# An attention and mixture-of-experts layer: rotation moved behind the q and k projections, and small uses moved to other slots

## The chip, the cores and the metric

The kernel runs on one core of one Trainium2 chip. The metric is the device time of one execution in microseconds. Three executions of the kernel before took 602.74, 608.37 and 611.11 us; their median is 608.37 us.

## The reference, cut to what matters

The input x has 8 batches of 512 tokens of width 128. One layer is differential attention with rotary positions, a residual sum and layer norm, then a top-1 mixture of 8 experts, a residual sum and layer norm.

```python
q = apply_rope((x @ Wq).reshape(B, T, 32, 4), cos, sin)      # x1*c + x2*s, -x1*s + x2*c
k = apply_rope((x @ Wk).reshape(B, T, 16, 4), cos, sin)      # halves of a head: d = 0,1 and 2,3
v = (x @ Wv).reshape(B, T, 8, 2, 4)
attn = softmax(q1 k1 / 2, causal) v - lambda_full * softmax(q2 k2 / 2, causal) v
attn = attn / rms(attn) * rms_w * (1 - LAMBDA_INIT)
x = layernorm(x + attn @ Wo)
max_prob, expert = top1(softmax(x @ router_w + router_b))
x = layernorm(x + max_prob * silu(x @ w1a[expert]) * (x @ w1g[expert]) @ w2[expert])
```

## The kernel before, in words

**Phases.** The attention part is a pipeline of `PHASES` = 34 phases. A phase g handles one group of head pairs, and four groups (`SUPER` = 4) make a batch, so phases come in fours: g%4 = 0, 1, 2, 3. A phase has nine slots t, each with two steps u. In each step TensorE writes one bank of scores in natural order for group g (`nat_mask`, `nat_part`, L681 and L699), whose row maxima VectorE takes (`row_max`, L1431), and one bank of transposed scores for group g-2 (`st_mask`, `st_part`, L718), which ScalarE turns into exponentials (`exp`, L980). In most slots the products with v follow (`pv`, L766). There are three banks for natural scores (`nat_b`), four for transposed ones (`st_b`) and one for the products with v (`pv_b`).

**Small uses.** At the end of a slot TensorE does what `uses(g, t)` lists, before that slot's `pv`. `PAIR_USES` come in every phase: `turn_max` in slot 2 (turns the row maxima, L803) and `turn_ot` in slot 4 (L809). `BATCH_USES` prepare the next batch b: q in two halves of 256 tokens ("q" in slot 6 and "q2" in slot 8 of phase 4b-4), k in two halves ("k" in slot 2 and "k2" in slot 6 of phase 4b-3), and v in slot 2 of phase 4b-2. `CHAIN` places the steps after the attention of a batch (output projection `wo`, `turn_x1`, `router`, `rank`, and GpSimd's `norm` and `sort`) as (phases after 4b, slot), and `JOBS` VectorE's small steps as (phases after 4b, step u, count).

**Rotation before.** GpSimd multiplies the transposed input `xt_s` by four rows of cosines and sines (`turn`, L1144, four products into `xr` in slots 0 to 3 of phase 4b-4). A half of q is then eight products on TensorE (`project`, L777 and L783): four column groups of 32, each the sum of a product with `wq_s[:, 2a]` and one with the weights of exchanged columns. ScalarE copies each half to `rot` (L1023). GpSimd splits `rot` into three bf16 parts (`split`, L1157 to L1163, slots 0 to 3: q in phase 4b-3, k in phase 4b-2). The SP queue writes the parts to `qk_parts` in DRAM (`write_part`, L533, six transfers per tensor) and reads them back as operands for each group (`operands`, `load_rows`, L548). It also sends the turned maxima out and in (`max_out` L568, `max_in` L575), all in one order per phase. The first batch is projected before the phases begin.

**Warm products.** In phases 0 and 1, and twice in phase 2, `warm_slot` adds products with no use of their own (L854, 512 columns) at the end of a slot: two per slot, none where a half of q or k stands.

**After phase 33** come the experts: 23 slots of rows with 256 x 128 products in f32 (`hidden` L909, `down` L924).

## Time and profile before

| | us |
|---|---|
| median of 3 executions (lowest, highest) | 608.37 (602.74, 611.11) |
| the profiled execution, its own time | 604.31 |
| its span, first to last instruction | 602.5 |
| TensorE busy | 573.8 (95%) |
| VectorE busy | 502.4 (83%) |
| ScalarE busy | 428.8 (71%) |
| GpSimd busy | 334.5 (56%) |
| mean granted clock of TensorE | 0.977 |

The busy time of TensorE contains the time in which a matmul passes through the array, so back-to-back products count as fully busy. Times of instructions are from the span's start. A phase is bounded here by the end of VectorE's last reduction of the phase (L1441); phase 0 begins at about 23.8 us and phase 31 ends at 455.7 us. The granted clock has two levels, 1.00 (2.4 GHz) and 0.50 (1.2 GHz).

### The profile page before, as it was taken

The numbers are of one execution on the slowest core, as the hardware profiler recorded it, in microseconds if no ns is written. First come the engines' busy times: TensorE is split into PE (matmuls) and PEld (weight loads), VectorE is DVE, ScalarE is ACT, GpSimd is POOL, SyncE is SP. The second block draws the span as 40 slices with busy tenths as digits, with TensorE's granted clock in tenths as the row PEclk, the third lists the DMA queues.
The fourth block names the chain that finished last, engine by engine and source line by source line (L and its number), as shares of the span: only waits on it lengthen the run. The fifth ranks groups of instructions, "written<-read, shape, count | busy, mean of one in ns | idle before, by whom it ended". The sixth has DMA issues, their size and how long they took to land.

```text
span 602.5 us, 30974 instructions
## 1 busy us (share of the span) xinstructions
PE 573.8 (95%) x12993; PEld 340.9 (57%) x13001; DVE 502.4 (83%) x1250; ACT 428.8 (71%) x903; POOL 334.5 (56%) x569
## 2 busy tenths in 40 slices
PE   7989999999999999999999999999999999999995
PEld 2434454555554555455445545555555588899995
DVE  4487898998999899899989998999996678866665
ACT  4115788998887888889888878889888845344443
POOL 5322033773577386739755773863265404866576
PEclk9977899999999999999999999999999999999998
DMA  3703312421341333234113412422110884698710
GB/s 107 188 10 111 101 36 77 119 54 35 92 113 41 88 94 90 57 85 116 41 50 91 117 43 76 107 68 57 35 26 24 277 262 153 208 316 260 256 56 35
DMA packets 44083, 62.85 MB, mean 104 GB/s; under 512 B 13436, under 2 KB 35196, under 8 KB 43800
## 3 DMA queue, kind: packets, MB, share of 16 engines
q1 hardware_dynamic: 38888, 54.31, 31.0%
q0 software_dynamic: 2416, 5.08, 2.4%
q8 instruction: 102, 1.67, 1.2%
q10 hardware_dynamic: 2640, 1.48, 1.0%
q14 instruction: 37, 0.30, 0.2%
HBM read 42.79 MB, written 21.65 MB: 107 GB/s over the span
## 4 chain that ended last, share of the span: by engine, by line
PE 56%; DVE 20%; POOL 15%; issue 6%; ACT 2%; DMA 1%; POOLq 0%; DVEq 0%; ACTq 0%
DVE mr L1431 14%; PE bank L766 13%; PE bank L909 9%; PE bank L681 7%; PE bank L699 7%; PE bank L924 4%; PE bank L777 3%; POOL x_all L1264 3%; PE bank L854 3%; PE bank L783 3%; PE bank L718 2%; PE bank L809 2%; PE bank L819 1%; PE bank L828 1%; POOL out_dram L1323 1%
## 5 line engine op out<-in xcount | busy, mean ns | idle before, releaser
L1431 DVE TENSOR_REDUCE mr<-bank 128x8 f32<-128x512 f32 x576 | 363.6, 681 | 43.5 <-PE bank L699 40.9
L980 ACT ACTIVATE work<-bank 128x512 f32<-128x512 f32 x576 | 313.1, 599 | 55.7 <-PE bank L718 49.4
L766 PE MATMUL bank<-work,v_aug 128*32 128x256 f32 (+6 forms) x2560 | 172.8, 370 | 0.0
L699 PE MATMUL bank<-kd,qd 24*64 24x192 bf16 (+7 forms) x2048 | 163.4, 289 | 0.0
L718 PE MATMUL bank<-qd,kd 27*64 27x320 bf16 (+7 forms) x2048 | 160.1, 286 | 0.0
L681 PEld LDWEIGHTS bank<-bits 32*64 32x64 bf16 x4608 | 76.7, 104 | 130.6 <-DVE mr L1431 63.5
L681 PE MATMUL bank<-bits 32*64 32x64 bf16 (+2 forms) x4608 | 131.4, 211 | 10.4 <-DVE mr L1431 7.0
L766 PEld LDWEIGHTS bank<-work,v_aug 128*32 128x32 f32 x2560 | 62.4, 110 | 58.3 <-issue 23.2
L1174 POOL CAST msplit<-mt 128x32 bf16<-128x32 f32 x32 | 6.8, 213 | 118.0 <-DVE mt L1441 118.0
L699 PEld LDWEIGHTS bank<-kd,qd 24*64 24x64 bf16 x2048 | 66.6, 109 | 0.1
L718 PEld LDWEIGHTS bank<-qd,kd 27*64 27x64 bf16 x2048 | 65.3, 108 | 0.0
L1100 ACT ACTIVATE sa<-bank 128x256 f32<-128x256 f32 (+1 forms) x92 | 30.9, 349 | 37.7 <-PE bank L909 29.6
L1276 POOL DMA_INDIRECT x_sorted<-x_all,pos_u x32 | 32.1, 1003 | 32.6 <-DVE pos_u L1521 25.1
L1323 POOL DMA_INDIRECT out_dram<-ynorm,row_u x39 | 39.4, 1009 | 11.9 <-issue 8.9
L1144 POOL TENSOR_TENSOR xr<-xt_s,rope 128x512 f32<-128x512 f32 x28 | 34.7, 1273 | 8.6 <-DMA xt_s<-in_xT 8.6
L1764 DVE TENSOR_TENSOR u_s<-sa,bank 128x256 f32<-128x256 f32 (+1 forms) x92 | 31.9, 375 | 7.4 <-ACT sa L1100 7.0
L909 PE MATMUL bank<-xr,wbuf 128*128 128x256 f32 (+1 forms) x176 | 35.5, 353 | 1.8 <-DVE xr L1720 0.7
L909 PE MATMUL bank<-xr,work 128*128 128x256 f32 (+1 forms) x192 | 37.1, 346 | 0.1
L909 PEld LDWEIGHTS bank<-xr,work 128*128 128x128 f32 x192 | 31.2, 191 | 3.4 <-DVE xr L1720 0.4
L909 PEld LDWEIGHTS bank<-xr,wbuf 128*128 128x128 f32 x176 | 29.1, 191 | 5.4 <-DVE xr L1720 1.1
L1082 ACT ACTIVATE ynorm<-ymix,shift,rstd 128x128 f32<-128x128 f32 x37 | 16.4, 486 | 19.8 <-DMA out_dram<-ynorm,row_u 15.7
L1333 POOL TENSOR_TENSOR rstd<-var,half 128x2 f32<-128x2 f32 (+1 forms) x23 | 15.5, 674 | 16.3 <-DVE var L1746 15.8
(206 smaller groups left out, 734.7 us busy)
## 6 DMA issues: line engine op xcount, KB each, us to landing
qk_parts<-parts SPq DMA_DIRECT2D x91, 128.0 KB, 2.4
work<-in_w SPq DMA_DIRECT2D x12, 768.0 KB, 6.1
wbuf<-in_w SPq DMA_DIRECT2D x11, 768.0 KB, 6.7
kd<-qk_parts SPq DMA_DIRECT2D x64, 96.0 KB
qd<-qk_parts SPq DMA_DIRECT2D x62, 96.0 KB
x_sorted<-in_c_pad SPq DMA_DIRECT2D x9, 390.0 KB, 4.6
xr<-x_sorted SPq DMA_DIRECT2D x16, 130.0 KB, 2.8
xt_s<-in_xT SPq DMA_DIRECT2D x8, 256.0 KB, 3.9
```

The lines of the kernel that those rows point to most:

```text
L681: pe.matmul(bk[L * c:L * c + L, :].rearrange("p (n t) -> p n t", t=L)[:, first:first + step * (wide - 1) + 1:step, cols], unit_h[lo:lo + L ...
L699: m = pe.matmul(bk[L * c:L * c + L, cols], qd[lo:lo + KROWS, s % 2, second, c, L * n:L * n + L], kd[lo:lo + KROWS, s % 2, second, c, 0:key ...
L718: m = pe.matmul(bk[L * c:L * c + L, cols], kd[lo:lo + KROWS + MAXROWS, s % 2, second, c, L * n:L * n + L], qd[lo:lo + KROWS + MAXROWS, s % ...
L766: m = pe.matmul(pv_b[32 * t:32 * t + 32, lo:hi], v_aug[:, vb, kv + v, kb, :], prob[:, pos, r, lo - back:hi - back], start=piece == 0, stop ...
L909: m = pe.matmul(banks[f][:, h * SLOT:h * SLOT + P * WIDE[j]], w_slots[j % WRING][:, h * FFN + f * P:h * FFN + (f + 1) * P], xst[:, n % 2, ...
L980: nc.scalar.activation(prob[:, pos, r, :], st_b[no % ST_RING][:, :], ACT.Exp, scale=HD ** -0.5).then_inc(s_sfree, 1)
L1100: nc.scalar.activation(sa[:, f, 0:P * WIDE[j]], banks[f][:, 0:P * WIDE[j]], ACT.Silu).then_inc(s_silu, 1)
L1144: nc.gpsimd.tensor_tensor(xr[:, i, :], xt_s[:, :], rope[:, i, :], ALU.mult).then_inc(s_xr, 1)
L1276: nc.gpsimd.indirect_dma_start(out=x_sorted, out_offset=bass.IndirectOffsetOnAxis(pos_u[:, n:n + 1], 0), in_=x1_all[:, n, :], in_offset=None)\
L1323: nc.gpsimd.indirect_dma_start(out=out, out_offset=bass.IndirectOffsetOnAxis(row_u[:, j, a:a + 1], 0), in_=ynorm[:, j % 2, a, :], in_offse ...
L1431: V.tensor_reduce(mr[:, s % 2, u % 2, i, i:i + NB], nat_b[no % NAT_RING][:, :].rearrange("p (n t) -> p n t", t=L), AX.X, ALU.max)\
L1764: V.tensor_tensor(u_s[:, j % 2, f, 0:cols], sa[:, f, 0:cols], banks[f][:, SLOT:SLOT + cols], ALU.mult)\
```

## The change

Q and k of a batch become one product each of the plain input `xt_s` (128 x 128 weights, 512 columns) in slot 2 (q in phase 4b-4, k in phase 4b-3), and one ScalarE copy to `rot`. `swap` on the SP queue copies `rot` with its two halves of 64 partitions exchanged to `xr`, in two transfers; `rotate` on GpSimd, in slot 4, multiplies `rot` by one row set, the exchanged copy by another, and adds them into `rot`. The columns of q and k are reordered so that an exchange of halves is the rotation's partner. The split of q stays in slots 0 to 3 of phase 4b-3; that of k moves to slots 5 to 8 of the same phase. The layout of `qk_parts` in DRAM changes with the columns. The four `turn` products on GpSimd go. `turn_attn`, `wo`, `turn_x1` go from slot 8 to 6, `norm` from 3 to 1, `rank` from 2 to 1, `sort` from 6 to 3, the jobs `stats` from step 17 to 14 and `place` from 8 to 4 (`rank`, `sort` and `place` stay as they were for batch 5, and batch 6 keeps its own table). Warm products become three per slot, five in the last slot of phase 0, and seven in phase 2: 57 in all for 30. Two products and two ScalarE copies at the start are set up for the new rows; two of the four old ScalarE copies go.

```diff
--- before.py
+++ after.py
@@ -61,13 +61,7 @@
 WARM_WAIT = 46
-def warm_slot(g, t):
-    if g < LAG:
-        return 0 if any(slot == t and (g - lag) % SUPER == 0 and g - lag >= SUPER for slot, _, lag in BATCH_USES) else 2
-    return 1 if g == LAG and t < 2 else 0
+WARM = [[3, 3, 0, 3, 3, 3, 3, 3, 5], [3, 3, 0, 3, 3, 3, 3, 3, 3], [3, 3, 1]]
@@ -128,13 +122,13 @@
 PAIR_USES = [(2, "turn_max", 1), (4, "turn_ot", 3)]
-BATCH_USES = [(6, "q", -4), (8, "q2", -4), (2, "k", -3), (6, "k2", -3), (2, "v", -2)]
+BATCH_USES = [(2, "q", -4), (2, "k", -3), (2, "v", -2)]
 FOR_DVE = ("wo", "router", "rank")
-CHAIN = {"turn_attn": (8, 8), "wo": (9, 8), "norm": (10, 3), "turn_x1": (10, 8), "router": (11, 2),
-         "chances": (11, 6), "rank": (12, 2), "sort": (12, 6)}
+CHAIN = {"turn_attn": (8, 6), "wo": (9, 6), "norm": (10, 1), "turn_x1": (10, 6), "router": (11, 2),
+         "chances": (11, 6), "rank": (12, 1), "sort": (12, 3)}
 CHAIN_SHORT = {"turn_attn": (8, 2), "wo": (8, 4), "norm": (8, 5), "turn_x1": (9, 1), "router": (9, 3),
@@ -144,8 +138,9 @@
-JOBS = {"guess": (7, 8, 3), "stats": (9, 17, 6), "choose": (11, 6, 8), "chance": (12, 0, 2),
-        "place": (12, 8, 3)}
+CHAIN_GROUP = {**CHAIN, "rank": (12, 2), "sort": (12, 6)}
+JOBS = {"guess": (7, 8, 3), "stats": (9, 14, 6), "choose": (11, 6, 8), "chance": (12, 0, 2),
+        "place": (12, 4, 3)}
 JOBS_SHORT = {"stats": (8, 9), "choose": (9, 7), "chance": (9, 12), "place": (9, 13)}
@@ -153,6 +148,8 @@
         for name, (lag, first, steps) in JOBS.items():
+            if b == B - 3 and name == "place":
+                first = 8
             if b == B - 2 and name in JOBS_SHORT:
@@ -167,7 +164,7 @@
     for b in range(B - 1):
-        lag, slot = (CHAIN_SHORT if b == B - 2 else CHAIN)[name]
+        lag, slot = {B - 3: CHAIN_GROUP, B - 2: CHAIN_SHORT}.get(b, CHAIN)[name]
         if (SUPER * b + lag, slot) == (g, t):
@@ -235,13 +232,13 @@
-        qk_parts = nc.dram_tensor("qk_parts", (B, 2, 2, SUPER * 2, TERMS, HD // 2, 4, T), BF16).ap()
+        qk_parts = nc.dram_tensor("qk_parts", (B, 2, TERMS, HD // 2, 2, SUPER * 2, 4, T), BF16).ap()
         max_rows = nc.dram_tensor("max_rows", (NS, 2, 3, 2, 2, NB, L), BF16).ap()
...
-        rope = sb("rope", [P, 4, T])
-        spread_s = sb("spread_s", [P, T + 4 * P], BF16)
+        rope = sb("rope", [P, 2, T])
+        spread_s = sb("spread_s", [P, T + 6 * P], BF16)
         ident = sb("ident", [P, P])
@@ -405,6 +402,8 @@
         s_xr = sem("s_xr")
+        s_swap = sem("s_swap")
+        s_rot = sem("s_rot")
         s_split = [sem("s_split_q"), sem("s_split_k")]
@@ -522,15 +521,18 @@
         PART_DONE = [1, 3, 4]
-        ROPE_ORDER, ROPE_BANK = [0, 2, 1, 3], [2, 3, 5, 6]
-        HALF = [slice(0, T // 2), slice(T // 2, T)]
+        ROPE_ORDER, ROPE_BANK = [0, 2, 1, 3], [2, 3, 5, 6, 7, 4]
+        def rotated(bn, a):
+            return 6 * (bn - 1) + 3 * a
...
                 if part == only:
-                    eng.dma_start(qk_parts[bn, a, :, :, term].rearrange("f x d w t -> (f x) (d w) t"),
+                    eng.dma_start(qk_parts[bn, a, term].rearrange("d f x w t -> (d f x w) t"),
                                   parts[:, a, part, :]).then_inc(done or s_written[a], 16)
@@ -546,7 +548,7 @@
                 eng.dma_start(dst[lo:lo + KROWS, s % 2].rearrange("p v j t -> p (v j t)"),
-                              qk_parts[s // SUPER, a, :, 2 * (s % SUPER) + r].rearrange("f m d w t -> (m d) f (w t)"))\
+                              qk_parts[s // SUPER, a, :, :, :, 2 * (s % SUPER) + r].rearrange("m d f w t -> (m d f) (w t)"))\
                     .then_inc(done, 16)
@@ -576,6 +578,13 @@
             sp.dma_start(xt_s[:, :], xT[:, 0]).then_inc(s_xt, 16)
+            def swap(bn, a):
+                wait(sp, s_sfree, ST_OUT[ST_NO["qk"[a], bn]])
+                for half in range(2):
+                    lo, other = P // 2 * half, P // 2 * (1 - half)
+                    sp.dma_start(xr[lo:lo + P // 2, 2 * a + 1, :], rot[other:other + P // 2, a, :]).then_inc(s_swap, 16)
@@ -603,6 +612,10 @@
                     max_out(g - 1)
+                for a in range(2):
+                    if batch_of(g, a - 4):
+                        swap(batch_of(g, a - 4), a)
+                if 0 <= g - 1 < NS:
                     max_in(g - 1)
@@ -638,7 +651,7 @@
                 weights(j)
-            wait(sp, s_st, ST_NO["k2", B - 1] + 1)
+            wait(sp, s_rot, rotated(B, 0))
             for j in range(NSLOT):
@@ -768,19 +781,17 @@
-            def project(a, bk, cols, first=False):
-                if first:
-                    wait(pe, s_xr, 2)
+            def project_first(a, bk):
+                wait(pe, s_xr, 2)
                 for c in range(4):
-                    lo, f = 32 * c, c // 2
-                    pe.matmul(bk[lo:lo + 32, cols], wq_s[:, 2 * a, lo:lo + 32], xr[:, 2 * f, cols], start=True, stop=False)
-                if first:
-                    wait(pe, s_xr, 4)
-                    wait(pe, s_sign, 16 + a + 1)
+                    lo, f = 32 * c, c % 2
+                    pe.matmul(bk[lo:lo + 32, :], wq_s[:, 2 * a, lo:lo + 32], xr[:, 2 * f, :], start=True, stop=False)
+                wait(pe, s_xr, 4)
+                wait(pe, s_sign, 16 + a + 1)
                 for c in range(4):
-                    lo, f = 32 * c, c // 2
-                    m = pe.matmul(bk[lo:lo + 32, cols], wq_s[:, 2 * a + 1, lo:lo + 32], xr[:, 2 * f + 1, cols], start=False,
+                    lo, f = 32 * c, c % 2
+                    m = pe.matmul(bk[lo:lo + 32, :], wq_s[:, 2 * a + 1, lo:lo + 32], xr[:, 2 * f + 1, :], start=False,
                                   stop=True)
@@ -844,8 +855,8 @@
                 else:
-                    wait(pe, s_xr, 4 * (n + 1))
-                    m = project("qk".index(name[0]), bk, HALF[len(name) - 1])
+                    wait(pe, s_xt, 16 * (n + 1))
+                    m = pe.matmul(bk[:, :], wq_s[:, 2 * "qk".index(name), :], xt_s[:, :], start=True, stop=True)
                 m.then_inc(done, 1)
@@ -854,18 +865,18 @@
             pe.wait_ge(s_rope, 16)
-            for n, i in enumerate(ROPE_ORDER):
+            for n, i in enumerate(ROPE_ORDER + [4, 5]):
                 pe.matmul(banks[ROPE_BANK[n]][:, :], spread_s[0:12, T + P * i:T + P * i + P], spread_s[0:12, 0:T],
...
             for a in range(2):
-                project(a, banks[a], slice(0, T), True).then_inc(s_first, 1)
+                project_first(a, banks[a]).then_inc(s_first, 1)
             pe.wait_ge(s_wv, 16)
+            pe.wait_ge(s_rows, 2)
             project_v(banks[4]).then_inc(s_first, 1)
...
             pe.wait_ge(s_vaug, 4)
-            pe.wait_ge(s_rows, 4)
             for a in range(2):
@@ -875,7 +886,8 @@
                         use(name, n)
-                    warm(warm_slot(g, t))
+                    if g < len(WARM):
+                        warm(sum(WARM[g][t:t + 1]))
                     if 0 <= g - LAG < NS:
@@ -1012,10 +1024,10 @@
                     dst, src = dt_s[:, :], bk[:, :]
-                elif name[0] in "qk":
-                    a, cols = "qk".index(name[0]), HALF[len(name) - 1]
+                elif name in "qk":
+                    a = "qk".index(name)
                     wait(act, s_split[a], 4 * n)
-                    dst, src = rot[:, a, cols], bk[:, cols]
+                    dst, src = rot[:, a, :], bk[:, :]
                 else:
@@ -1041,9 +1053,9 @@
-            for n, i in enumerate(ROPE_ORDER):
-                wait(act, s_xr, n + 1)
-                nc.scalar.activation(rope[:, i, :], banks[ROPE_BANK[n]][:, :], ACT.Copy).then_inc(s_rows, 1)
+            for i in range(2):
+                wait(act, s_spread, 4 + i + 1)
+                nc.scalar.activation(rope[:, i, :], banks[ROPE_BANK[4 + i]][:, :], ACT.Copy).then_inc(s_rows, 1)
             for a in range(2):
@@ -1136,19 +1148,22 @@
-            def turn(bn, i):
-                wait(pool, s_xt, 16 * (bn + 1))
-                if i == 0 and bn > 1:
-                    wait(pool, s_st, ST_NO["k2", bn - 1] + 1)
-                nc.gpsimd.tensor_tensor(xr[:, i, :], xt_s[:, :], rope[:, i, :], ALU.mult).then_inc(s_xr, 1)
+            def rotate(bn, a):
+                n = rotated(bn, a)
+                wait(pool, s_sfree, ST_OUT[ST_NO["qk"[a], bn]])
+                nc.gpsimd.tensor_tensor(xr[:, 2 * a, :], rot[:, a, :], rope[:, 0, :], ALU.mult).then_inc(s_rot, 1)
+                wait(pool, s_swap, 32 * (2 * (bn - 1) + a + 1))
+                nc.gpsimd.tensor_tensor(xr[:, 2 * a + 1, :], xr[:, 2 * a + 1, :], rope[:, 1, :], ALU.mult).then_inc(s_rot, 1)
+                wait(pool, s_rot, n + 2)
+                nc.gpsimd.tensor_tensor(rot[:, a, :], xr[:, 2 * a, :], xr[:, 2 * a + 1, :], ALU.add).then_inc(s_rot, 1)
...
                 if k == 0:
-                    wait(pool, s_sfree, ST_OUT[ST_NO[("q2", "k2")[a], bn]])
+                    wait(pool, s_rot, rotated(bn, a) + 3)
                 if k != 1:
@@ -1280,19 +1295,22 @@
             write_part(pool, 0, 1, 0, s_early)
-            pool.wait_ge(s_rows, 4)
+            pool.wait_ge(s_rows, 2)
...
                         split_max(g - 1)
-                    for a in range(2):
-                        b = batch_of(g, a - 3)
-                        if b and t < 4:
-                            split(b, a, t)
                     b = batch_of(g, -4)
+                    if b and t == 4:
+                        rotate(b, 0)
+                    b = batch_of(g, -3)
                     if b and t < 4:
-                        turn(b, t)
+                        split(b, 0, t)
+                    if b and t == 4:
+                        rotate(b, 1)
+                    if b and t > 4:
+                        split(b, 1, t - 5)
                     b = batch_of(g, 6)
@@ -1820,7 +1838,7 @@
-    f2, su, r, d2, v, j = np.meshgrid(range(2), range(SUPER), range(2), range(HD // 2), range(2), range(2), indexing="ij")
+    d2, f2, su, r, v, j = np.meshgrid(range(HD // 2), range(2), range(SUPER), range(2), range(2), range(2), indexing="ij")
     kv = 2 * su + v
@@ -1836,8 +1854,9 @@
     low = (rope - high.astype(f) - middle.astype(f)).astype(ml_dtypes.bfloat16)
-    to_rows = np.repeat(np.tile(np.eye(4), (3, 1)), P, 1).astype(ml_dtypes.bfloat16)
     sign = np.where(d.ravel() < 2, 1, -1)[None, :]
+    own = [(np.arange(4)[:, None] == 2 * f2.ravel()[None, :] + k) * (sign if k else 1) for k in range(2)]
+    to_rows = np.tile(np.concatenate([np.repeat(np.eye(4), P, 1)] + own, 1), (3, 1)).astype(ml_dtypes.bfloat16)
     before = (np.arange(P)[:, None] < np.arange(P)[None, :]).astype(f)
...
     upto = (np.arange(NX)[None, :] <= np.arange(NX)[:, None]).ravel()
```

## Rows read from the trace of the kernel before

**Rows 1.** The page, the span in 40 slices of 15 us: TensorE's granted clock in tenths.
```profile
PEclk9977899999999999999999999999999999999998
```
**Rows 2.** Busy time by stretch: phases 0, 1, 2, 5, 8, 16, 17 and 30.
```profile
core 0: us, PE busy (x) PEld busy (x) DVE busy (x) ACT busy (x) POOL busy (x), PEclk, DMA share, GB/s
23.80:35.31 11.51, 11.08 (x180) 5.08 (x182) 11.22 (x20) 0.00 (x0) 4.94 (x4) 1.00 0.46 109
35.31:52.44 17.13, 15.15 (x205) 5.71 (x206) 12.64 (x28) 2.45 (x8) 4.48 (x8) 0.70 0.32 90
52.44:67.77 15.33, 14.42 (x345) 6.96 (x342) 11.70 (x22) 11.13 (x24) 4.40 (x8) 0.67 0.31 82
...
91.49:104.64 13.15, 13.15 (x425) 6.67 (x421) 11.64 (x22) 11.62 (x24) 4.41 (x8) 1.00 0.34 87
...
129.37:141.78 12.41, 12.20 (x365) 6.51 (x361) 11.45 (x22) 11.07 (x23) 7.20 (x10) 1.00 0.16 40
...
238.38:252.27 13.89, 12.67 (x370) 6.62 (x366) 13.01 (x28) 11.36 (x23) 10.44 (x14) 1.00 0.17 48
252.27:267.08 14.81, 14.72 (x434) 7.67 (x437) 12.55 (x24) 11.91 (x24) 5.00 (x9) 1.00 0.37 93
...
428.98:442.44 13.46, 13.14 (x361) 6.77 (x361) 12.30 (x28) 11.19 (x22) 9.88 (x17) 0.87 0.18 49
```
**Rows 3.** Waits of phase 16, then of phase 17 (total us, times, longest).
```profile
PEld bank L681 <- DVE mr L1431: 3.7, 9, 0.7
...
DVE mr L1431 <- PE bank L699: 2.1, 3, 1.1
```
**Rows 4.** TensorE in order of time, phase 17: start, length, line, tiles, count.
```profile
256.12 0.26 PE L803 MATMUL bank<-bits,msplit 128*96 128x128 bf16 x1
...
257.30 0.33 PE L681 MATMUL bank<-bits 32*64 32x128 bf16 x12
...
261.41 0.64 PE L777 MATMUL bank<-xr,wq_s 128*32 128x256 f32 x8
...
262.30 0.56 PE L766 MATMUL bank<-work,v_aug 128*32 128x224 f32 x8
```
**Rows 5.** TensorE among the experts: eight f32 products of 256 columns, two records each.
```profile
540.16 3.62 PE L909 MATMUL bank<-xr,wbuf 128*128 128x256 f32 x16
543.62 0.38 PE L896 MATMUL bank<-ident,xr 128*128 128x128 f32 x2
```
**Rows 6.** TensorE in phase 0: two warm products, then the next scores.
```profile
26.20 0.61 PE L854 MATMUL bank<-bits 128*128 128x512 bf16 x2
26.74 0.27 PE L681 MATMUL bank<-bits 32*64 32x128 bf16 x4
```
**Rows 7.** TensorE's busy time by half microsecond, with the granted clock.
```profile
36.50:37.00 0.50, 0.00 (x0) 1.00 0.00 0
...
38.50:39.00 0.50, 0.50 (x16) 0.67 0.00 0
...
55.50:56.00 0.50, 0.50 (x6) 0.74 0.00 0
```
**Rows 8.** Groups by line and shape: GpSimd's product and its cast of 128x512.
```profile
L1144 POOL TENSOR_TENSOR xr<-xt_s,rope 128x512 f32<-128x512 f32 x28 | 34.7, 1273 | 8.6 <-DMA xt_s<-in_xT 8.6
...
L1161 POOL CAST parts<-rest 128x512 bf16<-128x512 f32 x14 | 8.6, 612 | 0.9
```
**Rows 9.** The job `place`: all eight, then one in phase 16 with GpSimd beside it.
```profile
L1516 DVE TENSOR_TENSOR place_f<-coded,chosen x8: 183/607/1194, 189.4 to 506.2; 128x32 f32<-128x32 f32 x8
...
244.57 1.18 DVE L1516 TENSOR_TENSOR place_f<-coded,chosen 128x32 f32<-128x32 f32 x1
...
240.75 4.96 POOL L1144 TENSOR_TENSOR xr<-xt_s,rope 128x512 f32<-128x512 f32 x4
```
**Rows 10.** Transfers of line 533 (128 KB each), and GpSimd's first instruction for phase 17.
```profile
DMA to landing us min/median/max: 2.3/2.6/3.8
...
252.86 0.22 POOL L1174 CAST msplit<-mt 128x32 bf16<-128x32 f32 x1
```

## The prediction

> **What bounds the kernel now.** I read four views. The page's slices of the granted clock come first: TensorE runs at its upper level but for the slices from 30 to 75 us [rows 1]. The busy time by phase comes second [rows 2]. Phases 1 and 2 take 17.1 and 15.3 us at a mean clock of 0.70 and 0.67; later phases take 12.4 to 14.8 us at 1.00. Phase 17, which projects k, has TensorE busy for 14.72 of 14.81 us and VectorE for 12.55: TensorE sets its length. Phase 5, of the same kind without an output projection, is full as well (13.15 of 13.15). Phase 16, which projects q, has VectorE busy for 13.01 of 13.89 us and TensorE for 12.67: here they alternate, VectorE ahead. The waits say the same [rows 3]: in phase 16 TensorE's weight loads wait 3.7 us for row maxima; in phase 17 VectorE waits 2.1 us for scores. GpSimd (10.44 and 5.00 us) and ScalarE (11.36 and 11.91) bound neither. The half-microsecond rows show how the clock falls [rows 7]: a stretch of no work at 36.5, and the lower level from within 38.5 to 39.0; it falls again within 55.5 to 56.0, when TensorE is busy all the time in those rows.
>
> **One product for two halves.** A half of k costs from its first product to the next work 262.30 - 261.41 = 0.89 us [rows 4]; the other half, with the turn of the maxima, 257.30 - 256.12 = 1.18 us. Two halves are 1.78 us. The new product is f32, 128 x 128 weights, 512 columns. Eight such of 256 columns take 543.62 - 540.16 = 3.46 us [rows 5], so one of 512 takes 2 x 3.46 / 8 = 0.87 us. Each of q and k saves 1.78 - 0.87 = 0.91 us of TensorE per batch.
>
> **Phases that project k** (5, 9, ... 25, six after the start) are bound by TensorE, so I give them 0.9 each: 5.4 us. The bounds are 0 (something else is as late) and 1.0 us each. After it phase 17 would take 13.9 us, still above VectorE's 12.55.
>
> **Phases that project q.** Four (12, 16, 20, 24) look like phase 16. TensorE falls from 12.67 to 11.8 us; that alone gives little, since VectorE has 13.01. But `place` moves from step 8 to step 4. Its first product took 1.18 us in phase 16, while GpSimd was in its four products (240.75 to 245.71), and 0.18 us at its best [rows 9]. In the new order GpSimd has no rotation before slot 4, so I expect 0.2 us, and VectorE falls to about 12.0 us. The phase then takes 12.8: 1.0 us less, 4.0 us over four. In phases 4 and 8 there is no `place`; phase 8 has VectorE at 11.45 of 12.41 us and TensorE at 12.20, so they fall to about 11.75: 0.65 each, 1.3 us. Together 5.3 us, with bounds 0 and 7.
>
> The row alone doesn't say that GpSimd is the cause. The Trainium skill ("SBUF — State Buffer", section "SBUF: two separate sides") says that a VectorE instruction with two SBUF inputs and a GpSimd instruction that reads SBUF exclude each other for their full length, the later one waiting. By that rule the 1.0 us goes with the move; without it VectorE keeps its 13.01 us, and the four phases fall to 13.3 at best: 2.4 us in place of 4.0. The trace agrees as far as it goes: the slow instance lies within GpSimd's row.
>
> **GpSimd.** Four products of 1.27 us per batch go; two times three come [rows 8]: 7.6 - 5.1 = 2.5 us more per batch. An exchange wait comes with each. In phase 16's kind the order is now the maxima, `sort` (about 5 us from slot 3), then the rotation of q, 3.8 us: it ends about 1.2 us after the phase. GpSimd then starts on the next maxima; in phase 17 that start is at 252.86, and the turn that needs it at 256.12 [rows 10, 4]. The four small instructions take some 1.1 us, so about 2.1 us are free and 1.2 late is covered. In the next phase GpSimd has the split of q (3.6), the rotation of k (3.8), the split of k (3.6) and the maxima (1.1): 12.1 of 13.9 us. Cost 0; if this cover fails, TensorE stands at the turn of the maxima, about 1 us in each of 12 phases.
>
> **The exchange** isn't in the trace. The nearest row is the 128 KB write to DRAM, 2.3 to 3.8 us to landing [rows 10]. I take 2.5. Behind it on the SP queue stands `max_in`, which is needed a phase later, and `write_parts`. GpSimd waits some 1 to 2 us for it in the rotation of k, and by the count above has as much to spare. Bounds: 0, and 1 us per exchange where late, 12 us. The other DRAM order moves the same rows in the same sizes: 0, bounds 1 us either way for the start.
>
> **ScalarE** makes one copy for two: 0. The start gets two more small products, hidden in the wait for the first multiplied input; the two fewer copies lie beside TensorE's work: 0. `stats`, `norm`, `wo` and `turn_x1` come earlier in phases with room; their sum is unchanged, and no end of a batch before the last sets the span: 0.
>
> **The warm products.** One takes about 0.21 us ((26.74 - 26.20) / 2 less the step over) [rows 6]. In phase 0 TensorE and VectorE both just fill a slot (11.08 and 11.22 of 11.51 us), so the third product makes TensorE the later: seven slots more by 0.2, and the last: +1.6 us. If the clock then stays up, phase 1 is 9 slots of 1.41 us (1.2 with the third product) and the turn and k: about 13.3 us, 3.8 less; phase 2 becomes like phase 8, 12.6 us, 2.7 less. The start gives 4.9 us. Bounds: all of it lost and 2 to 3 us paid, or 6 us gained. I take the gain because the dips follow thin stretches, and these products fill the thin stretches' neighbours.
>
> **Sum.** 5.4 + 5.3 + 4.9 = 15.6 us off the profiled execution's own 604.3 us: 588.7. The median of three is 4.1 us above that execution. I take this excess to be mostly clock, which the change may take away too, and leave a third: **590 us**.
>
> **The rivals.**
>
> The clock still falls at the start. For it: in the stall of 36.5 to 37.0, where VectorE sits in its constants after phase 0, the extra products cover only 0.6 us, and the seven of phase 2 stand in slots with scores. Against it: phase 0 held 1.00 with two per slot. Time: 604.3 - 10.7 + 2 = 595.6 us. The Trainium skill ("TensorE: Matmul & The Clock Gate", section "Part 1: The HAM clock gate") ties the fall to an idle engine; by that page products in busy slots would change nothing, and this case would be the forecast, at 596. Here the trace disagrees in part, with a fall in a row that is fully busy [rows 7].
>
> VectorE becomes the bound: phases with q keep their length but for 0.4 us each, so 5.3 becomes 2.4, and k phases give 0.6: 604.3 - 2.4 - 3.6 - 4.9 = 593.4 us. For it: VectorE's 13.01 of 13.89. Against it: phase 17's margin.
>
> GpSimd's queue is late, or the exchange lands late, and TensorE stands at the turn of the maxima by 1 us in 12 phases: 588.7 + 12 = 600.7 us. Against it: the 2.1 us free above.
>
> Slower: thinner phases lose the clock. Phase 30, which has neither q nor k, fell to a mean of 0.87 without a long stall [rows 2]. If in each of the 12 phases with q or k, now with less dense f32 work, TensorE fell for as long as at the start (some 10 us for 3.6 us of time, from phases 1 and 2), the time would be 588.7 + 43 = 632 us. From five such phases on the gain is gone. Against it: phases 5, 8, 16 and 17 all stand at 1.00.
>
> **How the numbers follow.** Chances: forecast 0.52, clock at the start 0.22, VectorE 0.12, GpSimd or exchange late 0.09, thin phases 0.05. A change of 2%, about what a measurement of this kernel can tell from none, is 596.2 or 620.5 us. The forecast lies below 596.2 in nine tenths of its cases (0.47), the clock case in half (0.11), the VectorE case in four fifths (0.10): faster 0.68. Within 2%: 0.28; slower: 0.04. The range 582 to 602 us takes in the upper bounds of the terms below, and the late GpSimd above.
>
> **What would show it.** Right: phases 13, 17, 21 at 13.9 us and 12, 16, 20 at 12.8; clock 1.00 in phases 1 and 2, at 13.3 and 12.6 us; `place` at 0.2 us; the maxima's first instruction within 2 us of the phase's start. Wrong: GpSimd waiting for the exchange until after its phase; a new wait of TensorE for `msplit`; VectorE at over 95% of phase 16; the clock's row below 1.00 in later phases.

## The result, and the profile after

The changed kernel takes 607.79 us (median of 20), the kernel before 603.94 us (median of 20, beside it): ratio 1.0085, 95% interval 1.0051 to 1.0118. The ratios here compare the means of those executions of each kernel that lie within 1.5% of its fastest, while the medians are of all of them. The change made the kernel slower by 0.9% (0.6% by the medians), which is little, but the interval leaves out 1; forecast were 590 us. Its profiled execution has a span of 607.7 us for 602.5.

The granted clock in 40 slices of 15.2 us, to be read against [rows 1]:

```profile
PEclk9985999799979999999999999999999999999999
```

The clock is still lost at the start, and now also in the slices from 106 to 122 us and from 167 to 182 us. These are phases 1, 2, 6 and 10 (phase 10 takes 16.6 us at a mean clock of 0.79); in the other phases the clock is 1.00. The busy time by stretch, as in [rows 2], for phases 1, 2, 6, 16, 17 and 18:

```profile
core 0: us, PE busy (x) PEld busy (x) DVE busy (x) ACT busy (x) POOL busy (x), PEclk, DMA share, GB/s
...
35.37:58.78 23.41, 17.27 (x176) 5.72 (x175) 12.73 (x28) 1.67 (x4) 15.41 (x18) 0.65 0.40 110
58.78:72.92 14.14, 13.52 (x364) 6.49 (x352) 11.76 (x22) 11.29 (x24) 0.91 (x4) 0.86 0.20 62
...
108.30:124.71 16.41, 14.27 (x373) 7.15 (x365) 11.77 (x22) 12.39 (x26) 9.10 (x15) 0.79 0.40 113
...
246.24:259.26 13.02, 12.72 (x376) 6.37 (x368) 12.16 (x28) 11.68 (x24) 7.71 (x12) 1.00 0.32 76
259.26:273.80 14.54, 13.56 (x379) 6.80 (x373) 12.90 (x27) 11.78 (x24) 12.00 (x15) 1.00 0.41 117
273.80:287.53 13.73, 12.54 (x373) 6.87 (x369) 11.89 (x26) 12.02 (x26) 12.06 (x20) 1.00 0.31 87
```

From the ends of all 32 phases the difference adds up so: phases 0 to 2 take 49.3 us for 44.2 (+5.1); phases 6 and 10 together 33.0 for 25.9 (+7.0); 14, 18, 22, 26 together 2.2 more; the six that project q 3.4 less; the six that project k after the start 3.3 less; phases 11, 15, 19, 23, 27 together 2.6 less; 28 to 31 0.7 less; what follows 0.8 more. That is +5.2, the difference of the spans. (Phase lengths here are taken from the exact end of the reduction; the bounds of the table above and of [rows 2] lie 0.2 us ahead of it.) Some 10 us were saved and 15 given back, most of it in phases 1, 6 and 10, where the clock fell.

How it was given back shows in GpSimd's rows at the start (start, length, and in brackets the idle time before and what ended it):

```profile
36.85 1.26 POOL L1155 TENSOR_TENSOR xr<-rot,rope 128x512 f32<-128x512 f32 x1 [21.48 <-ACT rot L1035]
39.81 1.27 POOL L1157 TENSOR_TENSOR xr<-xr,rope 128x512 f32<-128x512 f32 x1 [1.69 <-DMA xr<-rot]
41.15 1.26 POOL L1159 TENSOR_TENSOR rot<-xr 128x512 f32<-128x512 f32 x1
42.36 0.21 POOL L1189 CAST msplit<-mt 128x32 bf16<-128x32 f32 x1
...
43.26 0.25 POOL L1195 TENSOR_TENSOR msplit<-mrest,msplit 128x32 bf16<-128x32 f32 x1
```

The rotation of batch 1 waits 21.5 us for ScalarE's copy of q, and the maxima of group 0, ready at 35.6 us, stand behind it in GpSimd's order until 42.4. TensorE's rows by microsecond show what that does (stretch and its length, TensorE's busy time and count, granted clock, DMA share, GB/s):

```profile
38.00:39.00 1.00, 1.00 (x19) 1.00 0.96 205
39.00:40.00 1.00, 0.13 (x4) 1.00 0.78 215
40.00:41.00 1.00, 0.00 (x0) 1.00 0.78 184
41.00:42.00 1.00, 0.00 (x0) 1.00 0.13 33
42.00:43.00 1.00, 0.00 (x0) 0.63 0.00 0
...
62.00:63.00 1.00, 1.00 (x34) 0.63 0.00 0
```

TensorE stands for 4.4 us at the turn of the maxima (39.1 to 43.55 us), and its clock is half from 42.3 to 62.7 us. The copy is late because ScalarE's order has the exponential of lambda ahead of phase 0's copies, and it waits for VectorE's work at the end of phase 0:

```profile
35.87 0.20 ACT L1073 ACTIVATE lam_d<-lam_d 128x2 f32<-128x2 f32 x1 [18.95 <-DVE lam_d L1416]
36.10 0.60 ACT L1035 ACTIVATE rot<-bank 128x512 f32<-128x512 f32 x1
```

It stood there before too; then nothing needed the copy until phase 1. So the copy is not new, only GpSimd's wait for it ahead of the maxima. Later the same order bites less. At the change from phase 16 to 17 (259.26 us) GpSimd goes from `sort` into the rotation, and the maxima follow; the last row is TensorE's turn:

```profile
257.65 1.29 POOL L1155 TENSOR_TENSOR xr<-rot,rope 128x512 f32<-128x512 f32 x1
...
260.24 1.28 POOL L1159 TENSOR_TENSOR rot<-xr 128x512 f32<-128x512 f32 x1
261.46 0.21 POOL L1189 CAST msplit<-mt 128x32 bf16<-128x32 f32 x1
```
```profile
262.75 0.23 PE L814 MATMUL bank<-bits,msplit 128*96 128x128 bf16 x1 [0.77 <-ACT work L992]
```

The maxima start 2.2 us into the phase; TensorE is free at about 262.0 and goes on at 262.75, when their split, which ends at 262.6, is there. The wait is put down to ScalarE's `work`; the bank that the turn needs had been free since 260.7. In phases 6 and 10 the split of k stands ahead of the maxima as well, behind waits of 2.6 and 3.7 us for the exchange. The maxima start 3.3 and 2.7 us after the phase's start, and TensorE stands at their turn:

```profile
113.04 0.23 PE L814 MATMUL bank<-bits,msplit 128*96 128x128 bf16 x1 [2.02 <-POOL msplit L1195]
...
166.78 0.23 PE L814 MATMUL bank<-bits,msplit 128*96 128x128 bf16 x1 [1.36 <-POOL msplit L1195]
```

The clock is half for 6.8 us behind each (from 113.9 and from 168.6).

`place`, for [rows 9], is as forecast:

```profile
L1534 DVE TENSOR_TENSOR place_f<-coded,chosen x8: 181/182/194, 196.0 to 510.6; 128x32 f32<-128x32 f32 x8
```

### The profile page after: what moved, and what is told of

Read it like the earlier page. It is cut to its first block, busy times and chain, and to the rows that moved or that the text cites. A ratio compares the mean times of both kernels' runs of the same rounds, so it can differ in the third digit from the quotient of the medians.

```text
span 607.7 us, 30183 instructions
## 1 busy us (share of the span) xinstructions
PE 568.8 (94%) x12601; PEld 331.3 (55%) x12610; DVE 498.5 (82%) x1250; ACT 425.3 (70%) x887; POOL 353.5 (58%) x583
## 4 chain that ended last, share of the span: by engine, by line
PE 29%; DVE 16%; issue 4%; POOL 3%; ACT 1%; DMA 1%; DVEq 0%; POOLq 0%; ACTq 0%
DVE mr L1449 11%; PE bank L921 8%; PE bank L779 5%; PE bank L936 4%; PE bank L694 3%; PE bank L712 2%; PE bank L820 1%; PE bank L731 1%; PE bank L830 1%; POOL out_dram L1341 1%; PE bank L839 1%; PE bank L859 1%; DMA out_dram<-ynorm,row_u 1%; ACT work L992 1%; PE bank L908 1%
## 5 line engine op out<-in xcount | busy, mean ns | idle before, releaser
L712 PE MATMUL bank<-kd,qd 24*64 24x512 bf16 (+7 forms) x2048 | 161.9, 290 | 0.0
L694 PE MATMUL bank<-bits 32*64 32x64 bf16 (+2 forms) x4608 | 128.2, 212 | 7.5 <-DVE mr L1449 3.3
L779 PEld LDWEIGHTS bank<-work,v_aug 128*32 128x32 f32 x2560 | 61.1, 109 | 57.4 <-issue 23.1
L1341 POOL DMA_INDIRECT out_dram<-ynorm,row_u x39 | 39.5, 1012 | 11.5 <-issue 8.9
L1155 POOL TENSOR_TENSOR xr<-rot,rope 128x512 f32<-128x512 f32 x14 | 17.9, 1278 | 26.8 <-ACT rot L1035 26.7
L1157 POOL TENSOR_TENSOR xr<-xr,rope 128x512 f32<-128x512 f32 x14 | 17.9, 1275 | 21.8 <-DMA xr<-rot 21.8
```

The lines of the kernel that those rows point to most:

```text
L694: pe.matmul(bk[L * c:L * c + L, :].rearrange("p (n t) -> p n t", t=L)[:, first:first + step * (wide - 1) + 1:step, cols], unit_h[lo:lo + L ...
L712: m = pe.matmul(bk[L * c:L * c + L, cols], qd[lo:lo + KROWS, s % 2, second, c, L * n:L * n + L], kd[lo:lo + KROWS, s % 2, second, c, 0:key ...
L779: m = pe.matmul(pv_b[32 * t:32 * t + 32, lo:hi], v_aug[:, vb, kv + v, kb, :], prob[:, pos, r, lo - back:hi - back], start=piece == 0, stop ...
L1341: nc.gpsimd.indirect_dma_start(out=out, out_offset=bass.IndirectOffsetOnAxis(row_u[:, j, a:a + 1], 0), in_=ynorm[:, j % 2, a, :], in_offse ...
```

## Experiments

The theory: the change put GpSimd's rotation and the split of k ahead of the row maxima in GpSimd's fixed order; the maxima come late, TensorE stands at their turn, and the clock makes a short wait a long one. Rivals: the extra warm products, the landing of the exchange, the moved small uses. Ratios are to the kernel before on the same chip, with 95% intervals; phase lengths are from the profiled execution.

**e1, the exponential behind phase 0's copies.**
```diff
-            act.wait_ge(s_lam, 2)
-            nc.scalar.activation(lam_d[:, 2:4], lam_d[:, 0:2], ACT.Exp).then_inc(s_lexp, 1)
             for g in range(PHASES):
                 for t in range(NC):
+                    if g == 1 and t == 0:
+                        act.wait_ge(s_lam, 2)
+                        nc.scalar.activation(...)
```


> The changed kernel with one ScalarE instruction moved: the exponential of lambda, which waits for VectorE's work at the end of phase 0, stands behind phase 0's copies and no longer ahead of them. Theory: at the start the rotation of q waits for ScalarE's copy of q (21.5 us in the changed kernel), ends at 42.4 us, and the maxima of group 0 stand behind it on GpSimd's queue, so TensorE is idle for over 4 us and loses its clock. With q copied at about 27.5 us the rotation is over before phase 1: the maxima start at about 35.6 us, phase 1 takes 13 to 17 us for 23.4, TensorE has no idle stretch of over 2 us there, and the time is 6 to 10 us below the changed kernel's (598 to 602, ratio to before 0.985 to 0.995). Rival: the warm products or the stall in VectorE's constants set the clock; then phase 1 stays over 20 us and the ratio at 1.008.

603.75 us, ratio 0.9971 (0.9932 to 1.001). Phase 1 fell from 23.4 to 14.6 us as expected; phase 2 rose from 14.1 to 17.4 at a mean clock of 0.71, since the split of k stands ahead of its maxima. The split stood there in the changed kernel too, but phase 1 was long enough to hide it. TensorE waits 1.8 us at the turn of phase 2. Part of the start is explained, and the gain was under what I expected (598 to 602 us).

**e2, the maxima first.**
```diff
-                    b = batch_of(g, -4)
-                    if b and t == 4:
-                        rotate(b, 0)
                     b = batch_of(g, -3)
-                    if b and t < 4:
-                        split(b, 0, t)
-                    if b and t == 4:
-                        rotate(b, 1)
-                    if b and t > 4:
-                        split(b, 1, t - 5)
+                    if b and t == 0:
+                        rotate(b, 0)
+                    if b and 0 < t < 5:
+                        split(b, 0, t - 1)
+                    if b and t == 5:
+                        rotate(b, 1)
+                    b = batch_of(g, -2)
+                    if b and t < 4:
+                        split(b, 1, t)
```
(and `s_swap` is two semaphores, one per tensor)

> The changed kernel with GpSimd's order changed alone: the rotation of q stands behind the next phase's maxima, and the split of k behind the maxima of the phase after that (an own semaphore for each tensor's exchange). Theory that GpSimd's queue delays the turn of the maxima, at the start and in every batch: phase 1 falls from 23.4 to 13 to 18 us, phases 17 and 18 from 14.5 and 13.7 us to 13.7 and 13.0, phases 6 and 10 (16.4 and 16.6) to about 13, and the time is 12 to 18 us below the changed kernel's: 590 to 596, ratio 0.975 to 0.985. Rival: the late maxima matter at the start alone; then phases 17 and 18 stay and the ratio is 0.99 to 0.995. Rival: neither matters, the ratio stays at 1.008.

585.62 us (584.71 to 587.37), ratio 0.9684 (0.9634 to 0.9734), more than I expected (590 to 596 us). Phases 1, 2, 6, 16, 17, 18 of this kernel:

```profile
35.07:48.12 13.05, 12.15 (x178) 4.60 (x176) 12.39 (x27) 2.20 (x6) 10.55 (x13) 1.00 0.60 163
48.12:60.71 12.59, 12.09 (x350) 6.22 (x349) 11.54 (x21) 11.12 (x25) 5.76 (x10) 1.00 0.36 105
96.09:108.98 12.89, 12.45 (x369) 6.58 (x365) 11.68 (x21) 11.95 (x27) 10.03 (x16) 1.00 0.43 125
226.55:239.56 13.01, 12.71 (x372) 6.37 (x368) 12.17 (x27) 11.66 (x25) 5.95 (x9) 1.00 0.30 72
239.56:253.16 13.60, 13.40 (x383) 6.87 (x379) 12.90 (x26) 11.66 (x24) 11.93 (x14) 1.00 0.45 126
253.16:266.45 13.29, 12.53 (x363) 6.74 (x357) 11.90 (x25) 11.99 (x26) 12.48 (x19) 1.00 0.32 91
```

Every clock is 1.00. With the same work, the order of GpSimd alone takes 22 us off the changed kernel and makes it faster than the kernel before. GpSimd has as much to do in phase 17 as in the changed kernel (11.93 us for 12.00). The theory is shown, and the rival that the start alone matters is out: phases 17 and 18 fell too.

**e3, the warm products alone, on the kernel before.**
```diff
-        return 0 if any(...) else 2
-    return 1 if g == LAG and t < 2 else 0
+        if any(...):
+            return 0
+        return 5 if (g, t) == (0, NC - 2) else 3
+    return [3, 3, 1][t] if g == LAG and t < 3 else 0
```


> The kernel before with the larger number of warm products alone (three in a slot without a half of q or k, five in the last such slot of phase 0, seven in phase 2). Theory that the start went wrong by GpSimd's queue and not by these products: phase 0 grows by 0 to 2 us, phase 1 falls from 17.1 to 13 to 15 us if they hold the clock, and the ratio is 0.985 to 1.003. Rival, that they are what made the changed kernel slower: phases 0 to 2 together take over 46 us (44.0 before), ratio 1.005 or more.

600.12 us, ratio 0.9939 (0.9895 to 0.9983). Phases 0, 1 and 2:

```profile
23.80:37.69 13.89, 13.89 (x198) 5.41 (x194) 11.78 (x21) 0.00 (x0) 4.93 (x4) 0.88 0.36 92
37.69:51.12 13.43, 12.25 (x204) 4.91 (x202) 12.48 (x27) 2.43 (x8) 4.48 (x8) 1.00 0.34 92
51.12:63.35 12.23, 12.08 (x350) 6.22 (x349) 11.55 (x22) 11.00 (x25) 4.38 (x8) 1.00 0.36 99
```

39.6 us for 44.2. Phases 1 and 2 keep the full clock. Phase 0 grew by 2.2 us, but not by the products alone: its clock was half for 3.4 us (mean 0.88). Where the clock stayed up, in the changed kernel, phase 0 takes 11.9 us from its first row maximum, for 11.7 before. The extra products are not what made the changed kernel slower.

**e4, the changed kernel with the old warm products.**
```diff
-WARM = [[3, 3, 0, 3, 3, 3, 3, 3, 5], [3, 3, 0, 3, 3, 3, 3, 3, 3], [3, 3, 1]]
+WARM = [[2, 2, 0, 2, 2, 2, 2, 2, 2], [2, 2, 0, 2, 2, 2, 2, 2, 2], [1, 1]]
```


> The changed kernel with the old number of warm products (two in a slot, one in two slots of phase 2). Theory (GpSimd's queue): phase 1 stays at 20 to 24 us, since TensorE's idle stretch of 4 us is not filled by them; the ratio is 1.005 to 1.015. Rival (the extra products cost the start): phases 0 and 1 fall by 3 us or more and the ratio is about 1.00.

607.9 us, ratio 1.0052 (1.001 to 1.0094); phases 0, 1, 2 take 11.5, 21.2, 15.7 us. With the queue late, their number made no difference that can be told (1.0085 with them).

**e5, no exchange.** The two transfers per tensor are left out, and GpSimd's second product reads the copy that is not exchanged; q and k come out wrong.
```diff
-                wait(pool, s_swap, 32 * (2 * (bn - 1) + a + 1))
-                nc.gpsimd.tensor_tensor(xr[:, 2 * a + 1, :], xr[:, 2 * a + 1, :], rope[:, 1, :], ALU.mult)...
+                nc.gpsimd.tensor_tensor(xr[:, 2 * a + 1, :], rot[:, a, :], rope[:, 1, :], ALU.mult)...
...
-                        swap(batch_of(g, a - 4), a)
```


> The changed kernel without the exchange of halves: the two transfers per tensor are left out and GpSimd's second product reads the unexchanged copy, so q and k of batches 1 to 7 are not rotated rightly; the three GpSimd instructions per tensor stay. Theory that the order on GpSimd is what costs, with the transfer only a part of the lateness: the rotation of k ends 1.7 to 2.6 us earlier, so phases 18, 22, 26 get their maxima in time, but the rotation of q still stands ahead of the maxima: phase 17 keeps about 14.5 us, phase 1 falls by about 2 us only and keeps its clock loss; ratio 0.995 to 1.004. Rival, that the exchange's landing is the cause: phases 1, 17 and 18 fall to 13 to 13.6 us and the ratio to about 0.97.

593.14 us, ratio 0.9846 (0.9763 to 0.9928), a larger gain than I expected. Phase 1 takes 18.6 us for 23.4, phases 6 and 10 12.9 and 13.3 for 16.4 and 16.6, phase 18 13.3; phase 17 keeps 14.5. The wait for the exchange thus costs where the split of k stands behind it and ahead of the maxima; the late rotation of q costs by itself in phases 1 and 17.

**e6, the slots alone, on the kernel before.**
```diff
-CHAIN = {"turn_attn": (8, 8), "wo": (9, 8), "norm": (10, 3), "turn_x1": (10, 8), ... "rank": (12, 2), "sort": (12, 6)}
+CHAIN = {"turn_attn": (8, 6), "wo": (9, 6), "norm": (10, 1), "turn_x1": (10, 6), ... "rank": (12, 1), "sort": (12, 3)}
-JOBS = {... "stats": (9, 17, 6), ... "place": (12, 8, 3)}
+JOBS = {... "stats": (9, 14, 6), ... "place": (12, 4, 3)}
```
(with the exceptions for batch 5 as in the change)

> The kernel before with the other slots and steps for the small uses alone (turn_attn, wo, turn_x1, norm, rank, sort, stats, place). Theory that VectorE's place product waited for GpSimd's four products: they still stand in slots 0 to 3 of the phase, and place now comes at step 4, within them, so it stays slow (about 1 us), and the phases with q keep 13.4 to 13.9 us; ratio 0.995 to 1.003. Rival, that the move by itself gave the phases with q their 0.8 us: phases 12, 16, 20 take about 13.0 us, ratio about 0.993.

623.59 us, ratio 1.0345 (1.0274 to 1.0417): both expectations were too mild. Phases 12, 16, 20, 24 took 17.0 to 18.6 us for 13.7 to 13.9. In phase 16, VectorE's steps 4 and 6 of `place`, and what GpSimd did beside them:

```profile
250.67 0.93 DVE L1519 TENSOR_TENSOR place_f<-coded,chosen 128x32 f32<-128x32 f32 x1
...
252.81 1.22 DVE L1524 CAST pos_u<-pos_f 128x4 uint32<-128x4 f32 x1
```
```profile
249.05 4.96 POOL L1147 TENSOR_TENSOR xr<-xt_s,rope 128x512 f32<-128x512 f32 x4
```
```profile
252.00:253.00 1.00, 0.56 (x20) 1.00 0.08 12
253.00:254.00 1.00, 1.00 (x19) 0.69 0.08 12
```

Two small steps within GpSimd's products took 2.15 us (the cast takes 0.15 us elsewhere, the product 0.18), TensorE ran short, and its clock was half for 6.8 us (last two rows: TensorE by microsecond). With the four products gone, in e2, the same slots give these phases 13.0 us. For the product with two inputs this agrees with the rule of the Trainium skill that the prediction cites from "SBUF — State Buffer": the later of the two instructions waits for the other's full length. It is not the slower rival of the prediction: that had phases lose the clock because their work is less dense, and here it fell behind a stall.

**e7, e1 and e2 together.** The edit is the sum of both.

> The maxima first on GpSimd (e2) and also the exponential of lambda behind phase 0's copies (e1). Theory that one order repairs it: with the rotation behind the maxima the copy of q at 36 us is early enough, so nothing is added: phases as in e2 within 0.3 us each, ratio 0.965 to 0.972. Rival, that the late copy still costs in phase 1: phase 1 falls by 1 us or more and the ratio is 0.002 or more below e2's 0.968.

585.92 us, ratio 0.9772 (0.9727 to 0.9817), beside e2's 585.62; phase 1 takes 13.05 us in both. The two ratios differ by the runs of before beside them, not by the kernels' own medians. The late copy costs nothing once the maxima do not stand behind it.

**e8, no rotation.** Rotation and exchange are left out for batches 1 to 7, with the waits for them.
```diff
-                        rotate(b, 0)
...
-                        rotate(b, 1)
...
-                        swap(batch_of(g, a - 4), a)
```


> The changed kernel with the rotation and the exchange left out for batches 1 to 7 (q and k stay unrotated), the order of the rest unchanged. It is the bound for what the projection, the slots and the warm products give when GpSimd has 7.6 us less per batch. Theory: phases as in e2 (13.0 for 16, 13.6 for 17, 13.3 for 18, 13.0 and 12.6 for 1 and 2) and 584 to 588 us, ratio 0.965 to 0.972, so that e2 has hidden the rotation wholly. Rival, that the rotation costs even in e2's order: this one is 3 us or more below e2's 585.6.

585.41 us, ratio 0.9786 (0.9717 to 0.9856); phases 1, 2, 16, 17, 18 take 13.05, 12.2, 13.0, 13.6, 13.3 us. e2 hides the rotation wholly.

**e9, e2 with the old warm products.** The edit is that of e4 on e2.

> The kernel with the maxima first on GpSimd (e2) and the old number of warm products (30 for 57). If the extra products hold the clock at the start: phases 1 and 2 take 15 to 17 us at a clock below 1.00, and the time is 4 to 7 us over e2's 585.6 (590 to 593, ratio 0.975 to 0.982). Rival, that the repaired queue alone holds the clock: phases 0 to 2 take no more than 38 us and the ratio is 0.965 to 0.970.

594.94 us, ratio 0.9865 (0.9802 to 0.9927). Phases 1 and 2:

```profile
35.41:52.37 16.96, 15.43 (x166) 4.69 (x164) 12.67 (x27) 1.77 (x5) 11.92 (x14) 0.60 0.55 150
52.37:68.45 16.08, 15.92 (x347) 7.75 (x346) 11.82 (x21) 11.74 (x25) 4.38 (x8) 0.58 0.28 80
```

With the queue repaired, the 27 extra products are worth 9.3 us. They hold the clock; the repaired queue alone does not.

**e10, the split of k back.** The changed kernel's order, with `split(b, 1, t)` in slots 0 to 3 of phase 4b-2.

> The changed kernel with the split of k alone moved back behind the maxima of the following phase; both rotations stay in slot 4. Theory: phases 18, 22, 26 fall to 13.3 us and keep the clock, phases 6 and 10 fall from 16.4 and 16.6 us to about 13, while phase 1 (over 20 us) and phase 17 (14.5) stay: the time is 5 to 9 us below the changed kernel's (ratio 0.993 to 1.000). Rival, that the late rotation of q costs all of it: phases 6 and 10 stay over 16 us and the ratio at 1.005 or more.

599.52 us, ratio 0.9936 (0.9889 to 0.9982). Phases 6 and 10: 12.9 and 13.3 us; phase 1: 23.35; phase 17: 14.45. As expected.

**e11, the rotation of q alone behind the maxima.** The split of k stays in slots 5 to 8.

> The changed kernel with the rotation of q alone moved behind the next phase's maxima; the split of k stays in slots 5 to 8 of the same phase. GpSimd then has maxima, rotation, split, rotation, split in a row in phases 4b-3: about 1.1 + 3.8 + 3.6 + 3.8 + 3.6 = 15.9 us and any wait for the exchange. Theory: phase 17 falls from 14.5 to 13.6 us, but the next maxima start 2.5 us or more into phase 18, so phases 2, 6, 10, 18 take 14 to 17 us and lose the clock in several: ratio 1.000 to 1.015, no better than the changed kernel. Rival (the rotation of q is the whole cost): phase 18 at 13.3 us, ratio 0.970 to 0.980.

617.15 us, ratio 1.0273 (1.0199 to 1.0347), worse than I expected (1.000 to 1.015). Phase 17 fell to 13.6 us, and phases 2, 6, 10, 14, 18, 22, 26 took 16.6 to 19.6, each with a fall of the clock. Its wait at the turn of the maxima (total us, times, longest):

```profile
PE bank L814 <- POOL msplit L1195: 16.2, 8, 4.3
```

Half of the repair is worse than none: the late work moved from one phase to the next.

**e12, the maxima late in the kernel before.**
```diff
+                    if t == 0 and (batch_of(g, -3) or batch_of(g, -2)):
+                        for _ in range(3):
+                            wait(pool, s_mt, 2 * g)
+                            ...
+                            nc.gpsimd.tensor_tensor(idle[:, :], rope[:, 0, :], rope[:, 1, :], ALU.mult)...
                     if t == 0 and 0 <= g - 1 < NS:
                         split_max(g - 1)
```


> The kernel before with three GpSimd products of no use (128x512, about 1.27 us each, into a tile of their own) between the end of the row maxima and their split, in phases 4b-3 and 4b-2 alone. They make those maxima start about 4.1 us into the phase and end at 5.3, where the turn is due at about 3.8. Theory that a late start of the maxima on GpSimd is by itself enough: phases 17 and 18 grow by 1 to 2 us each, some phases lose the clock, and the ratio is 1.02 to 1.06. Rival, that lateness on GpSimd is covered elsewhere: under 0.3 us per phase, ratio under 1.008.

655.59 us, ratio 1.0924 (1.0864 to 1.0984). Its wait for the maxima, and phases 17 and 18:

```profile
PE bank L806 <- POOL msplit L1183: 32.9, 15, 2.9
```
```profile
286.55:304.82 18.27, 16.14 (x433) 7.85 (x429) 12.63 (x23) 12.11 (x25) 8.55 (x12) 0.91 0.32 80
304.82:322.05 17.23, 14.57 (x373) 8.21 (x367) 12.41 (x27) 12.62 (x26) 16.07 (x22) 0.80 0.31 86
```

The maxima start 4.1 to 4.6 us into the 14 phases, and TensorE stands for 2.3 us at the turn on average (1.1 to 2.9), not the 1.5 that I had worked out. The 14 phases grow by 50 us in the profiled execution, 3.6 each, about twice what I expected; the medians differ by 48.5. (Phase 0, which the edit does not touch, also grew, by 4.6 us at a lower clock; phase 30 shrank by 1.3.) In phase 17 VectorE is busy for 12.63 us, for 12.55 before, so the added products do not act by slowing it. Late maxima are enough by themselves, in a kernel without any other part of the change.

## Why the prediction was wrong

**The step that failed** is the one on GpSimd: "about 2.1 us are free and 1.2 late is covered ... Cost 0". Four parts of it were off.

- The lateness. My 1.2 us put `sort` at 5.2 us into the phase (12.8 + 1.2 - 3.8 - 5.0); it waits for `place` and begins at 252.70, 6.5 us in. So the rotation ended at 261.5 and the maxima began 2.2 us late.
- The cover. I read the 2.1 us from the kernel before, whose turn stands at 256.12, 3.85 us into phase 17. In the changed kernel TensorE is there 2.7 us in: the change itself takes `turn_attn` and the second half of q out of the last slot of phase 16, so TensorE comes to the turn sooner. In e6, where only `turn_attn` has left that slot, it is 3.1 us by the same bounds. A start 1.2 us late would just have been covered; 2.2 was not, and TensorE stood for 0.8 us. e10 and e2 price it: phase 17 takes 14.5 us with the rotation ahead of the maxima and 13.6 behind. In e2, where the maxima of phase 17 are in time, the turn comes 2.4 us after the phase's start at 239.56:

```profile
242.00 0.26 PE L814 MATMUL bank<-bits,msplit 128*96 128x128 bf16 x1
```

- The exchange. I gave its wait "some 1 to 2 us" in the rotation of k, with "as much to spare", since 12.1 us of work stood in a phase of 13.9. There were ten waits, 21.8 us in all and up to 4.2; in phases 5 and 9 they were 2.6 and 3.7 us, and phase 5 lasts only 11.9 us, so there was no spare. e5: phases 6 and 10 fall by 3.5 and 3.3 us without it.
- The first batch. I worked out phase 16's kind and took the start for the same. ScalarE's copy of q came at 36 us before as well; the change made GpSimd wait for it ahead of the maxima. e1: phase 1 falls from 23.4 to 14.6 us.

**The price of lateness** in the rival of a late GpSimd, 1 us per phase and 600.7 us in all, was right in part. In phases 13, 17, 21 and 25 of the changed kernel TensorE stood for 0.8 to 1.0 us, kept its clock, and each cost 0.9 to 1.1 us against e2. Where it stood longer the clock fell, which the rival left out: 1.4 and 2.0 us in phases 10 and 6 cost 3.3 and 3.5, and 4.4 us in phase 1 cost 10.4. Phases 1, 2, 6 and 10 hold 18.7 of the 22 us between the changed kernel and e2.

**What held**, read from e2, where TensorE waits at this turn for 0.8 us in all. The product for two halves and the phases with k: 1.2 us less (14.8 to 13.6) for the 0.9 I gave; the six gave 7.1 us for 5.4. The phases with q: 13.0 for a forecast 12.8, together 3.4 us for 5.3; phases 4 and 8, for which I gave 1.3, gave 0.2. `place` at 0.18 us. The warm products: phases 1 and 2 at 13.05 and 12.6 us for 13.3 and 12.6; phases 0 to 2 gave 7.3 us for 4.9, because phase 0 paid 0.2 us for them and not 1.6, and because it began 0.65 us sooner in this execution, which no term has. e9 shows that these products hold the clock. The sum was 15.6 us; e2 gives 604.3 - 585.6 = 18.7. The mechanisms on TensorE and VectorE stood; that their sum comes so near is in part luck, since it was too low for k and the start and too high for q. The answer turned on a queue that bounds nothing by its share (58%).

**Of the rivals**, the late GpSimd had a chance of 0.09; it is what happened, with the start's clock loss as its consequence and not, as the rival on the clock at the start had it, in spite of the products. The signs that I had named for it came: a new wait of TensorE for `msplit`, and the clock below 1.00 in later phases. The slower rival, that thin phases lose the clock, is out by e2, where all 12 phases with q or k stay at 1.00. The sum that goes by the Trainium skill's rule on shared ports ("SBUF — State Buffer", "SBUF: two separate sides") was the right one of the two for `place`. For the fall of the clock, the rule of the Trainium skill ("TensorE: Matmul & The Clock Gate", "Part 1: The HAM clock gate") that ties it to an idle engine fits the stretch from 39.1 to 43.55 us. What the prediction drew from it, that products in busy slots change nothing, did not hold: 594.9 us in e9 without the extra ones, 585.6 in e2 with them.

**Open.** Why phases 11, 15, 19, 23 and 27 are 0.5 us shorter in the changed kernel was not tried alone. The traces point to the same queue. In the kernel before, the maxima start 1.6 us into these phases, behind GpSimd's work on the batch just finished, and TensorE waits 0.2 us for them: 13.6 us. In e2 and e6 they start at 1.2 to 1.3: 13.2 us. In the changed kernel they start at 0.07: 13.05 us. Open too is why the phases with k gave 1.2 us and not 0.9, and what made the clock fall in e3 and e12 early in phase 0.

## What to carry to other kernels

When a step moves on an engine with a fixed order, lay out that engine's rows for the phase, with every wait, up to the next instruction that someone else waits for, and do it for the first batch too. Take the moment at which it is needed from the changed kernel: a change that frees the waiting engine brings that moment forward. An engine at 58% can set the time by one small instruction behind a long one. Put the short instruction that others need first, and the long private ones behind it.

## What the runs showed of the hardware

A short stall of TensorE can cost far more than itself. TensorE stood for 2.0 us to 113.04, its clock was half for the 6.8 us from 113.9, and phase 6 took 3.5 us more than in e2; a stall of 4.4 us at the start was followed by 20 us at half clock. It need not: four stalls of 0.8 to 1.0 us in the changed kernel left the clock at 1.00 and cost about their own length, while in e4 stalls of 0.9 and 0.8 us in phases 13 and 26 were followed by half clock and cost 2.5 us each. In e6 the clock fell at 253.4 us, behind a microsecond with 0.56 us of work in it. And a VectorE cast with one small input took 1.22 us for 0.15 while GpSimd was in its products, and the product with two inputs 0.93 for 0.18.
